# Weight preparation one pair earlier, one power for the normalisation, the first table made before the second part, and five closing slots in a decoder layer on one core

## What is computed

```python
q, k, v = x @ Wq.T + bq, x @ Wk.T + bk, x @ Wv.T + bv          # 16 heads of 32
fourier = lambda h: concat([cos(p), sin(p)]) / sqrt(128)        # p = h @ proj_mat / sqrt(32)
kv = einsum('blhm,blhd->bhmd', fourier(k), v)
x = layernorm(x + einsum('blhm,bhmd->blhd', fourier(q), kv).reshape(...) @ Wo.T + bo)

h = rmsnorm(x, g_res) @ W_in.T + b_in
table = decaying sum over the 64 rows of rmsnorm(ctx, g_init)[:, :512]
x = layernorm(x + h + table[patch of this row])                 # patches end where cumsum(lens) says

x = layernorm(x + fp6_quantised(x) @ fp6_quantised(W_ffn).T + bias)   # blocks of 32 share a scale
```

## Time and profile before

| what | value |
|---|---|
| three runs | 1681.5, 1679.65, 1676.27 us |
| the profiled execution | 1677.72 us, its span 1675.9 us |
| PE busy | 1606.7 us (96% of the span), granted clock 0.984 in the mean |
| DVE, ACT, POOL busy | 71%, 69%, 42% |
| first part | from 0 to 1199.8 us |
| second part | from 1200.2 us to the end |
| closing slots | about 1625.8 to 1675.9 us |

### The profile page before, as it was taken

One profiled execution on the slowest core, in us unless ns is written; L12 is line 12 of the kernel. 1 busy time (PEld: TensorE's weight loads), 2 busy tenths in 40 slices (PEclk: granted clock), 3 DMA queues, 4 the chain that ended last, 5 costly groups with the idle time before them and its releaser, 6 DMA issues. The chain is left out here.

```text
span 1675.9 us, 31880 instructions
## 1 busy us (share of the span) xinstructions
PE 1606.7 (96%) x12212; PEld 1151.2 (69%) x12212; DVE 1187.6 (71%) x1831; ACT 1151.1 (69%) x1518; POOL 711.5 (42%) x668
## 2 busy tenths in 40 slices
PE   6999999999999999999999999998789999999995
PEld 5756776676676667667667766754467887788884
DVE  5577667657757766876776686788577777777774
ACT  5697778778777867867777786678145656665664
POOL 2033106203411520340241053346268888897886
PEclk8999999999999999999999999999799999999998
DMA  4100202200210220120022022001612222222211
GB/s 168 52 26 1 77 1 77 76 2 18 84 52 1 77 77 1 54 91 9 2 76 76 2 77 76 27 26 50 161 32 82 76 83 82 81 75 82 76 41 60
DMA packets 49183, 95.88 MB, mean 57 GB/s; under 512 B 3552, under 2 KB 3872, under 8 KB 49056
## 3 DMA queue, kind: packets, MB, share of 16 engines
q1 hardware_dynamic: 38944, 76.29, 14.4%
q10 hardware_dynamic: 10112, 17.69, 2.9%
HBM read 60.38 MB, written 33.59 MB: 56 GB/s over the span
## 5 line engine op out<-in xcount | busy, mean ns | idle before, releaser
L762 DVE SCALAR_TENSOR_TENSOR feat<-feat,phases 128x1024 f32<-128x1024 f32 x256 | 301.1, 1218 | 195.6 <-ACT feat L655 195.4
L655 ACT ACTIVATE feat<-phases 128x1024 f32<-128x1024 f32 x256 | 248.3, 1024 | 141.5 <-PE phases L508 120.0
L662 ACT ACTIVATE feat<-feat 128x1024 f32<-128x1024 f32 x256 | 271.8, 1062 | 66.4 <-DVE feat L762 57.5
L380 POOL TENSOR_TENSOR xt_hi<-xt_raw,zero 128x512 fp32r<-128x512 f32 x60 | 69.6, 1189 | 537.1 <-PE bank L499 507.9
L668 ACT ACTIVATE feat<-feat 128x1024 f32<-128x1024 f32 x256 | 255.7, 1047 | 2.7 <-DVE feat L769 2.7
L769 DVE TENSOR_SCALAR feat<-feat 128x1024 int32<-128x1024 int32 x256 | 197.3, 774 | 47.0 <-ACT feat L662 46.7
L393 POOL TENSOR_TENSOR res<-res,bo_all 128x512 f32<-128x512 f32 x60 | 72.2, 1227 | 182.7 <-DMA res<-x 182.4
L596 PE MATMUL kv_sum<-feat,kv_cols 128*32 128x512 f32 x1024 | 124.1, 602 | 0.0
L570 PE MATMUL kv_sum<-feat,v 128*32 128x256 f32 x2048 | 123.8, 382 | 0.0
L1222 ACT ACTIVATE xs<-xs,shift,rstd 128x512 f32<-128x512 f32 x96 | 71.4, 806 | 67.8 <-POOL shift L1097 67.8
L497 PE MATMUL bank<-xt_hi,win_hi 128*128 128x512 f32 x256 | 108.9, 426 | 7.6 <-DVE win_lo L711 7.6
(11 more groups left out here) (209 smaller groups left out, 3964.0 us busy)
## 6 DMA issues: line engine op xcount, KB each, us to landing
normed<-res SPq DMA_DIRECT2D x32, 513.0 KB, 4.0
xt_raw<-xT SPq DMA_DIRECT2D x15, 1024.0 KB, 7.0
res<-x SPq DMA_DIRECT2D x30, 512.0 KB, 4.2
xs<-normed SPq DMA_DIRECT2D x24, 513.0 KB, 3.8
out<-xs ACTq DMA_DIRECT2D x24, 512.0 KB, 2.8
feat<-normed SPq DMA_DIRECT2D x8, 513.0 KB, 3.8
out<-feat ACTq DMA_DIRECT2D x8, 512.0 KB, 2.8
xt_raw<-ctx SPq DMA_DIRECT2D x8, 256.0 KB, 3.5
```

The lines of the kernel that those rows point to most:

```text
L655: act.activation(feat[2 * (w % 2) + p][:, 0, :], phases[:, 2 * p:2 * p + 2, :].rearrange("p h n -> p (h n)"), ACT.Identity, bias=ROUND).th ...
L662: act.activation(f[:, 1, :], f[:, 0, :], ACT.Sin, scale=-TWO_PI).then_inc(sin_done, 1)
L762: dve.scalar_tensor_tensor(f[:, 0, :], f[:, 0, :], ROUND, phases[:, 2 * p:2 * p + 2, :].rearrange("p h n -> p (h n)"), ALU.subtract, ALU.s ...
```

## The change

Five edits.

1. In the batch `last`, `weight_peaks`, `weight_steps` and `weight_ties` hang on the steps `cos(2)` to `cos(7)` in place of `cos(3)` to `cos(8)`, and `residual_weight` moves from `tail` to directly behind `quantise_weight`.
2. `powers` has five steps. DVE makes one instruction more in `stats` (`ln[:, 0]` from the variances, so that the scale is a single power of it), `norm` waits for that one power only, and SP waits for all five before a store.
3. The first batch's table is made in `tail`: ACT squares the context behind its last `wf`, POOL takes the power between the last two `powers`, DVE makes the patch behind W(1, 1), PE the product behind W(1, 3), and DVE and ACT finish the table around the last `norm`. In slot 0 `select`'s square, `patch` and `table` go.
4. The closing has five slots. `back` comes four slots behind and `ffn` five; slot 0 holds `lin` for pair 31 with its own `norms`, and the bias addition is an entry of its own behind `norms` or `means`.
5. The context loads of the second part wait for one patch fewer.

The core of the diff:

```diff
@@ attention_steps
-        15: [..., norm(0, 1), ("ends",), W(1, 0),
-             ("repeats",), W(1, 1), W(1, 2), W(1, 3), stats(1), norm(1, 0), norm(1, 1)],
+        15: [..., norm(0, 1), ("ends",), W(1, 0),
+             ("repeats",), W(1, 1), ("context",), W(1, 2), W(1, 3), stats(1), ("table",), norm(1, 0), norm(1, 1), ("parts",)],
@@ sync, attention
             def store(k, last=False):
+                sp.wait_ge(ln_step, LN_STEPS * (k + 1))
                 for h in range(HALVES):
@@ powers
-                pool.wait_ge(moments_done, k + 1)
-                step(1, pool.tensor_tensor(shifted, var, eps[:, 0, :], ALU.add))
-                step(2, pool.tensor_tensor(rstd, shifted, half_power[:, 0, :], ALU.pow))
...
-                step(7, pool.tensor_tensor(scale, rstd, inv, ALU.mult))
+                pool.wait_ge(var_ready, k + 1)
+                pool.tensor_tensor(scale, spread_var, half_power[:, 0, :], ALU.pow).then_inc(ln_step, 1)
+                pool.tensor_tensor(shifted, var, eps[:, 0, :], ALU.add).then_inc(ln_step, 1)
+                pool.tensor_tensor(root, spread_var, half_power[:, 1, :], ALU.pow).then_inc(ln_step, 1)
+                pool.wait_ge(ln_step, base + 3)
+                pool.tensor_tensor(rstd, shifted, half_power[:, 0, :], ALU.pow).then_inc(ln_step, 1)
+                pool.wait_ge(ln_step, base + 4)
...
@@ gpsimd, batch
                 if mode == "tail":
                     add_last_bias()
-                    residual_weight(i - 1)
                     powers(2 * i - 2)
+                    pool.wait_ge(squared, 1)
+                    pool.tensor_tensor(shifted_square[:], mean_square[:], rms_eps[:], ALU.add).then_inc(context_scaled, 1)
+                    pool.wait_ge(context_scaled, 1)
+                    pool.tensor_tensor(context_inv[:], shifted_square[:], minus_half, ALU.pow).then_inc(context_scaled, 1)
                     powers(2 * i - 1, last=True)
...
                 else:
                     quantise_weight()
+                    residual_weight(i)
@@ tensor
+                    elif kind == "table":
+                        pe.wait_ge(patch_ready, 1)
+                        pe.wait_ge(ends_step, 1)
+                        pe.matmul(out_part[0], kept.decay[:], patch, start=True, stop=True).then_inc(table_done, 1)
@@ scalar
+                    elif kind == "context":
+                        act.wait_ge(kept.context_in, 16)
+                        act.wait_ge(win_split, KD)
+                        act.activation(squares, context, ACT.Square, scale=DCTX ** -0.5, accum_out=mean_square[:]).then_inc(squared, 1)
+                    elif kind == "parts":
+                        act.wait_ge(table_read, 1)
+                        act.activation(table_parts, table, ACT.Identity).then_inc(table_hi, 1)
@@ vector
-                    if mode == "last" and s == ("cos", 3):
+                    if mode == "last" and s == ("cos", 2):
                         weight_peaks()
...
+                        dve.wait_ge(moments_done, k + 1)
+                        dve.tensor_scalar(ln[:, 0, :], moments[:, :, 1], 1.0 + RMS_EPS, LN_EPS * RMS_EPS, ALU.mult, ALU.add).then_inc(var_ready, 1)
                     elif kind == "norm":
                         k = 2 * own + s[1]
-                        dve.wait_ge(ln_step, LN_STEPS * (k + 1))
+                        dve.wait_ge(ln_step, LN_STEPS * k + 1)
...
+                    elif kind == "context":
+                        dve.wait_ge(context_scaled, 2)
+                        dve.wait_ge(constants_in, 16 * 3)
+                        dve.scalar_tensor_tensor(patch, context[:, 0:D], context_inv[:], kv_cols[0:PATCHES, 1, :], ALU.mult, ALU.mult).then_inc(patch_ready, 1)
+                    elif kind == "table":
+                        dve.wait_ge(table_done, 1)
+                        dve.tensor_tensor(table, out_part[0], kv_cols[:, 0, :], ALU.add).then_inc(table_read, 1)
+                    elif kind == "parts":
+                        dve.wait_ge(table_hi, 1)
+                        low = slice(PATCHES, P)
+                        dve.tensor_tensor(table_parts[low, :], table[low, :], table_parts[low, :].bitcast(F32), ALU.subtract)
@@ slot_order
-            [("select",), ("turn", 0), ("patch",), ("count",), ("table",), ("choose",), ("turn", 1), ("means",), ("norms",)],
+            [("select",), ("turn", 0), ("count",), ("turn", 1), ("choose",), ("means",), ("norms",)],
...
     if mode == "tail":
         return (
-            [("quant",), ("scale",), ("lin", 0), ("lin", 1), ("ffn", 0), ("ffn", 1), ("means",), ("back", 0),
-             ("back", 1), ("norms",)],
-            [("quant",), ("scale",), ("ffn", 0), ("ffn", 1), ("norms",), ("means",), ("back", 0), ("back", 1)],
-            [("quant",), ("ffn", 0), ("ffn", 1), ("means",), ("back", 0), ("back", 1), ("norms",)],
-            [("ffn", 0), ("ffn", 1), ("norms",), ("means",)],
+            [("quant",), ("lin", 0), ("lin", 1), ("means",), ("scale",), ("norms",), ("bias",)],
+            [("ffn", 0), ("ffn", 1), ("back", 0), ("back", 1), ("scale",), ("quant",), ("means",), ("bias",), ("norms",)],
+            [("ffn", 0), ("ffn", 1), ("back", 0), ("back", 1), ("quant",), ("means",), ("bias",), ("norms",)],
+            [("ffn", 0), ("ffn", 1), ("back", 0), ("back", 1), ("means",), ("norms",)],
+            [("ffn", 0), ("ffn", 1), ("means",), ("norms",)],
         )[s]
@@ slot_steps
-    lag = {"lin": LIN, "scale": SCALE, "quant": QUANT, "back": BACK, "ffn": FFN}
+    late = 1 if mode == "tail" else 0
+    lag = {"lin": LIN, "scale": SCALE, "quant": QUANT, "bias": QUANT, "back": BACK + late, "ffn": FFN + late}
@@ context_and_quantised, norms_of
+            if mode == "tail":
+                return [(LIN, 0)] if s == 0 else [(FFN + 1, PAIR)]
```

## The result

The changed kernel takes 1687.36 us, the median of four runs (1686.73 to 1689.87), the kernel before 1677.96 (1675.94 to 1681.5, four runs, three of them those shown above). The ratio is 1.0054, with a 95% interval of 1.0039 to 1.0070: slower, by 9.1 us. The profiled executions have 1686.73 and 1677.72 us, 9.0 apart, so that they can be read against each other.

A forecast was written before the change was run, and what follows sets the result against it. PE was taken to bound the kernel, losing time only at pair 8, pairs 14 and 15, the block's end and the closing. -2.2 - 2.8 + 1.4 + 13.6 = +10.0 on 1677.7, plus 1.9 for the median: 1689.5 us (1681.5 to 1695).

The forecast's parts named there:

- cost and give nothing: Middle of the first part: shorter powers, DVE's added instruction and SP's longer wait change nothing, as engines other than PE have slack.
- A: Pair 8 of the last batch: weight steps one pair earlier shrink PE's stalls, 2.2 us gained (0.9 to 3.6).
- this gives 0.9 us if the clock still falls ... 3.6 us: Pair 8: low half ends earlier, 0.9 us gained; 3.6 if PE also avoids its lower clock level.
- at nothing: Price of the weight steps a pair earlier, covered by PE's products in hand; without cover, 2.7 us again.
- B: Pairs 14 and 15: with residual_weight gone both stalls shrink, 2.8 us gained (2.3 to 3.3).
- C: First part's end and slot 0: one power and the table made ahead, a loss of 1.4 us (0.7 to 2).
- 1204.9 ... the block ends 5.1 us later: End of the first part: SP's last store ends at 1204.9, before at 1199.79, as DVE's patch waits for the context.
- D: Five closing slots: inputs of pairs 29 to 31 come later, last store 13.6 us late (11.5 to 15.5).
- R4: Rival: POOL and DVE hold one another up in pairs 8, 9 and the closing, +14.3 us, 1694; chance 0.13.
- R1: Rival: the closing gains, pair 31's scale starting 3 to 5 us sooner, -5 in place of +13.6, 1671; chance 0.10.
- the ring: Closing: back_hi copies wait behind ACT's normalisation, its power behind POOL's work; pair 30 6.7 us late, pair 31 11.1.
- R2: Rival: the context lands before W(1, 1) is added, at 1186.8, block ends 2 us sooner, 5.4 gained, 1682.7; chance 0.09.

The follow-up runs named there:

- loads_sorted: context_late with SP issuing the context, g_init, b_in and the row of positions first, the first pairs of normed last: 1667.04 us, ratio 0.9917.
- best: ctx_first with the bias addition of closing slot 1 behind that slot's power instead of with the quantisation (four closing slots): 1676.64 us, ratio 0.9975.
- ab_alone: The kernel before with only the weight steps one pair earlier and residual_weight behind quantise_weight: 1673.91 us, ratio 0.9964.
- pow_alone: The kernel before with only the one power (new powers, stats, norm and SP's wait): 1673.98 us, ratio 0.9966.
- norms_first: The changed kernel with POOL taking the layer norm's power ahead of the bias addition in closing slots 1 and 2: 1684.94 us, ratio 1.0025.
- abpow: The kernel before with both weight moves and the one power; the first table stays in slot 0, the closing has four slots: 1668.33 us, ratio 0.9933.
- d_alone: The kernel before with only the five closing slots: 1694.79 us, ratio 1.0083.
- a_alone: The kernel before with only the weight steps a pair earlier; residual_weight stays in pairs 14 and 15: 1675.68 us, ratio 0.9978.
- ctx_first: old_closing with SP issuing the first context's load first, not last, of the loads at the end of the first part: 1673.14 us, ratio 0.9959.
- old_closing: The changed kernel with the four closing slots of the kernel before; all its other edits stay: 1674.34 us, ratio 0.9964.
- power_early: The changed kernel with means and norms directly behind the two ffn in closing slots 1 to 3: 1682.54 us, ratio 1.0023.
- context_late: old_closing with DVE's context patch behind the last two W products' additions and stats, the table's addition behind the last normalisation: 1668.49 us, ratio 0.9938.

## Why the prediction came out right

**What bounds the kernel.** Right as to the places, but the main loop wasn't neutral. From DVE's first feat behind 305 us to that behind 1020 us it took 716.3 us before and 718.8 in the changed kernel. Of the ten profiled kernels with the one power eight lie between 718.5 and 719.3 (loads_sorted has 717.2, best 720.4), the four without it between 716.3 and 718.0. So "cost and give nothing" was wrong by some 1.6 us in the mean, though the two groups touch. PE waited 12.0 us for `stack_lo` from 60 to 1030, 9.5 before, and DVE's wait and its added instruction stand ahead of that operand; but ab_alone, without the one power, has 11.1 too, as pow_alone has. No run took that instruction out alone, so the cause isn't shown.

**A.** The step "this gives 0.9 us if the clock still falls ... 3.6 us" had its upper end right, and that one came: the products behind the stall of 1.91 us ran at 0.40, not 0.63, and A is -3.8. The stall before the low half did not shrink (1.91 for 1.51); what went is the stall of 2.32. In ab_alone the clock fell for a while (0.97 in the mean over 1100 to 1150) and A was 2.2; norms_first has 2.4 and loads_sorted 2.2, the other seven kernels with both moves 3.8, all behind the same stall of 1.91 to 1.93. So the lower end was too low, and the middle that I took is what happens when the clock falls. The move wasn't free either where I priced it "at nothing": a pair earlier PE now waits 0.86 us for `res`, where it had no wait over 0.2 before, since the weight steps stand ahead of DVE's addition. The folds of pairs 8 and 9, 2.44 and 2.73 us for two, and one of pair 14 answer to the earlier trace rows:

```profile
1110.58 2.44 DVE L789 TENSOR_SCALAR feat<-feat 128x1024 int32<-128x1024 int32 x2
...
1117.44 2.73 DVE L789 TENSOR_SCALAR feat<-feat 128x1024 int32<-128x1024 int32 x2
...
1155.93 0.69 DVE L789 TENSOR_SCALAR feat<-feat 128x1024 int32<-128x1024 int32 x1
```

**B.** Right in the waits: 0.96 and 0.76 where 0.8 was said, with folds of 0.69 in pair 14. B is -3.6, over its bound of 3.3; behind the second pause PE worked at the upper level, a granted clock of 1.00 from 1165 to 1180, where it had been 0.87 and 0.79 over 1170 to 1180 before. The forecast read the low level from the row of 0.63 at 1172.30, which doesn't show it: four transposes take 0.63 us at the upper level (1161.67 in the same rows, and both rows above), and 1.08 at the lower. And B is the stretch whose length varies most: with the instructions of before it took 70.98, 73.73, 72.53 and 70.51 us in four profiles, with both moves 67.3 to 67.8 and once 69.12.

**C.** The context landed 8.9 us after its issue at 1178.12 (forecast 9.0), and the opening gave back 3.4 us (6.41 to 2.98; forecast 3.5). The failed step is "1204.9 ... the block ends 5.1 us later": it ended 4.0 later against the last W product (13.86 us from its start to the first transposes, 9.84 before). From the squares' start to the table's matmul it took 2.87 us and not 3.24, the context's issue came 0.2 us earlier against the W products, and SP issued its two last stores in 0.91, not 1.25. The forecast's own sum also has a slip: 5.1 less 3.5 is 1.6, not 1.4. C is +0.6 here, below its bound of 0.7; in the three other kernels with the same instructions up to there it is +0.9, +1.1 and +1.4, within the range. Taken apart by the runs it is two things of opposite sign in this stretch, a power that gives 2.3 (14.00 against 16.25) and a table's move that costs 2.9 (16.84 against abpow's 13.99), and the forecast's C didn't see the 1.5 to 2.6 us that the move costs between the first store and pair 27's.

**The clock behind the second batch's table.** No term of the sum had it. PE at the table's two matmuls and at a 128x512 matmul soon behind them, in the kernel before, in ab_alone and in the changed kernel:

```profile
1235.31 2.07 PE L1163 MATMUL table_sum<-patch,decay_sb 64*128 64x512 f32 x2 [2.41 <-DVE patch L1263]
1239.51 0.63 PE L1123 MATMUL bank<-win_lo,turn_hi 128*128 128x512 f32 x1
```

```profile
1230.54 1.12 PE L1163 MATMUL table_sum<-patch,decay_sb 64*128 64x512 f32 x2 [2.41 <-DVE patch L1263]
1233.02 0.63 PE L1123 MATMUL bank<-win_lo,turn_hi 128*128 128x512 f32 x1
```

```profile
1229.85 1.12 PE L1201 MATMUL table_sum<-patch,decay_sb 64*128 64x512 f32 x2 [2.38 <-DVE patch L1302]
1232.07 0.39 PE L1161 MATMUL bank<-win_lo,turn_hi 128*128 128x512 f32 x1
```

PE had waited 2.4 us each time. There are three outcomes. The low level begins at the table in before, d_alone, a_alone, ctx_first and best, and the opening is 56.0 to 56.2 us. It begins 1.9 us behind the table's start and is shorter in ab_alone, abpow and norms_first, with 53.4 to 53.5. The clock stays up in the changed kernel, pow_alone, old_closing, power_early, context_late and loads_sorted, with 51.7 to 52.4; only the changed kernel itself has 53.6, since POOL's power ahead of that first store took 2.0 us there, 1.3 in old_closing. So a gain of 2.6 to 4.5 us comes and goes with no term of its own. What decides it stays open; none of the five edits does by itself, since ctx_first and old_closing have the same of them and differ in the order of loads alone.

**D.** Right, with the term too small by 1.7. Counted from pair 27's store, pair 29's copy starts after 6.35 us (forecast 6.4), pair 30's first product after 25.8 (24.3), pair 31's after 40.7 (39.2), the last store after 55.0 (53.4). Nearly all of the miss arises between the first two, where POOL's scaling of pair 31 now lies beside DVE's quantisation of pair 30:

```profile
1637.17 1.41 DVE L1341 TENSOR_SCALAR grid<-grid 128x1024 f32<-128x1024 f32 x1
1638.62 1.95 DVE L1343 TENSOR_TENSOR quantised<-scaled,grid 128x1024 f32<-128x1024 f32 x1
```

```profile
1636.67 2.82 POOL L1124 TENSOR_TENSOR scaled<-xs,inv 128x512 f32<-128x512 f32 x2 [2.73 <-DVE inv L1322]
```

They take 0.69 and 1.23 us in a later slot, alone; the two extra 0.72 are the 1.4 that pair 30 is late by. R4's mechanism was there once, not in each slot. The Trainium skill ("SBUF — State Buffer", "Who interferes with whom") has DVE, in a 2-port mode or with two SBUF inputs, and GpSimd exclude each other on one port pair. The rows agree as far as both lengthen when they overlap: 1.41 for 0.69, and 2.82 for 2.06 on POOL. They don't tell whether the later one was blocked for the whole of the other's instruction.

**The rivals.** R1 fails: pair 31's scale did start early (1634.78, 8.2 us after pair 27's store, 11.6 before), and the ring took it back. R2 fails: the context was not early, and with its load first the patch stood for `g_init` instead, at the same time.

## What to carry to other kernels

Follow what a step stands behind on each engine's queue, not how early its inputs are: here an earlier normalisation made the copy behind it late, and a table made ahead held two sums for the last load of a burst. The loads of this burst took 7.1 to 9.8 us to land, with no clear gain from standing first: sort such loads by need, and check what is last. Two instructions that stretch one another on DVE and POOL can be brought together by an edit far away: ask at each place which of the two PE waits for. Measure a stage between two marks of its own when totals of the same code differ by 2 us: the closing of four slots took 39.69 to 39.75 us in eight kernels, and the ninth, pow_alone with 41.34, could then be traced to the clock.

## What the runs showed that I had not expected

The same instructions up to pair 27's store brought profiles of 1626.61, 1630.48 and 1629.20 us there (the changed kernel, norms_first, power_early), the latter two 1.3 and 2.4 us behind already at the last batch and 2.9 at the last W product. Each profile lies within 0.8 us of its own kernel's median, but the executions of each kernel spread over 3.1, 5.2 and 6.8 us, so these three profiles don't tell whether the difference stays with a kernel or with an execution.
